# Four buffers for a head's exponentials, and the class key's column copied for two heads at once

## The reference

```
AC = einsum('bqhd,bkhd->bhqk', q + u, k)
BD = einsum('bqhd,khd->bhqk', q + v, kr)
prob = softmax((AC + BD) * inv_sqrt_d, axis=-1)
vec = einsum('bhqk,bkhd->bqhd', prob, val).reshape(b, s_len, H * DH)
h = layer_norm(h + vec @ W_o[i], ln1_g[i], ln1_b[i])
ff = relu(h @ W_ff1[i] + b_ff1[i]) @ W_ff2[i] + b_ff2[i]
h = layer_norm(ff, ln2_g[i], ln2_b[i])
```

## Time and profile before

| what | value |
|---|---|
| median of 3 runs | 2653.75 us (2649.84 to 2658.7) |
| the profiled execution's own time | 2649.49 us |
| its span | 2647.7 us |
| mean granted TensorE clock | 0.968 |
| busy: PE, DVE, ACT, POOL | 84%, 70%, 61%, 45% |
| calls of line 1676 | 512 |

### The profile page before, as it was taken

How to read it: one execution, slowest core, us unless ns; L and a number is a source line. 1 busy time by engine, 2 the same in 40 slices (tenths; PEclk the granted TensorE clock), 3 DMA queues, 4 the chain that set the end, 5 groups by cost and what they waited for, 6 DMA issues and landing times. The chain is left out here.

```text
span 2647.7 us, 61352 instructions
## 1 busy us (share of the span) xinstructions
PE 2226.1 (84%) x19254; PEld 1636.3 (62%) x19254; DVE 1844.0 (70%) x5666; ACT 1611.5 (61%) x5073; POOL 1188.7 (45%) x2205
## 2 busy tenths in 40 slices
PE   0159999999988999999899999999899989972998
PEld 0136666666766666667666666676666666651565
DVE  8837777777767777777677777777677777773333
ACT  2136666666666677676666777666576666661222
POOL 3025555555556555545565555545455555511011
PEclk9679999999999999999999999999999999996999
DMA  4344444445554444455544444546444444406110
GB/s 162 95 124 115 110 106 106 106 117 135 138 153 118 107 105 107 103 145 140 148 122 103 101 105 106 122 131 183 109 95 102 102 103 93 97 24 205 49 41 27
DMA packets 378062, 295.38 MB, mean 112 GB/s; under 512 B 45087, under 2 KB 350721, under 8 KB 376739
## 3 DMA queue, kind: packets, MB, share of 16 engines
q1 hardware_dynamic: 370603, 272.41, 41.5%
q10 hardware_dynamic: 4864, 12.68, 1.4%
q0 software_dynamic: 2272, 6.35, 0.7%
HBM read 137.71 MB, written 72.07 MB: 79 GB/s over the span
## 5 line engine op out<-in xcount | busy, mean ns | idle before, releaser
L1654 ACT ACTIVATE E<-E,nb 128x257 f32<-128x257 f32 x1024 | 517.3, 518 | 40.8 <-DVE nb L1837 40.2
L1837 DVE CUSTOM_DVE_ANT_0 E<-bk,cb 128x257 f32<-128x257 f32 x1024 | 390.3, 419 | 75.3 <-PE bk L1447 73.9
L1354 PE MATMUL bk<-hin,w_sb 128*128 128x257 f16 x3072 | 423.9, 275 | 11.8 <-ACT rel L1589 7.0
L1799 DVE TENSOR_TENSOR pt<-bk,pt 128x512 f16<-128x512 f32 x512 | 353.9, 691 | 77.0 <-ACT pt L1639 70.2
L1402 PE MATMUL bk<-ident,E 128*128 128x128 f32 x2048 | 324.1, 281 | 68.4 <-ACT E L1654 52.5
L1354 PEld LDWEIGHTS bk<-hin,w_sb 128*128 128x128 f16 x3072 | 298.0, 98 | 62.7 <-issue 10.3
L1402 PEld LDWEIGHTS bk<-ident,E 128*128 128x128 f32 x2048 | 220.4, 141 | 156.7 <-ACT E L1654 135.5
L1639 ACT ACTIVATE pt<-bk 128x512 f16<-128x512 f32 x512 | 311.3, 608 | 6.9 <-PE bk L1402 6.9
L1290 POOL TENSOR_SCALAR wf<-wf 128x256 f32<-128x256 f32 x216 | 93.9, 435 | 426.7 <-DMA wf<-in_w_dram 258.2
L1446 PE MATMUL bk<-kh,qs 128*128 128x257 f16 x1024 | 255.2, 275 | 10.8 <-DMA kl<-rk 10.6
L1240 POOL TENSOR_SCALAR rq<-rel 128x257 f16<-128x257 f32 x248 | 101.3, 409 | 342.3 <-ACT rel L1589 342.3
(11 more groups left out here) (303 smaller groups left out, 4474.7 us busy)
## 6 DMA issues: line engine op xcount, KB each, us to landing
qs<-rq SPq DMA_DIRECT2D x256, 128.5 KB
kh<-rk SPq DMA_DIRECT2D x256, 128.5 KB
kl<-rk SPq DMA_DIRECT2D x256, 128.5 KB
wf<-in_w_dram SPq DMA_DIRECT2D x168, 128.0 KB, 2.9
w_split_dram<-wh SPq DMA_DIRECT2D x168, 128.0 KB, 2.2
xs_dram<-in_c_blank_dram SPq DMA_DIRECT2D x24, 772.5 KB
w_sb<-w_split_dram SPq DMA_DIRECT2D x18, 1024.0 KB, 15.2
wf<-in_we_dram SPq DMA_DIRECT2D x96, 128.0 KB, 2.6
```

The lines of the kernel that those rows point to most:

```text
L1354: r_ = mm(bank[4 + s % 2][:, 0:S], wcol(a, C_QKV, k, 3 * HD, chunk_at(s)), hin[:, m, k, :], start=i == 0, stop=i == 5)
L1654: act.activation(E[:, h % 2, qt, :], E[:, h % 2, qt, :], ACT.Exp, bias=nb[:, 2 * h + qt:2 * h + qt + 1], scale=-1.0, accum_out=sums[:, qt, ...
L1799: v.tensor_tensor(pt[:, h, 1, :, 0:IMG], bank[2 + h % 2][:, :].rearrange("p (k s) -> p k s", k=QT), pt[:, h, 0, :, 0:IMG], ALU.subtract).t ...
L1837: v.tensor_tensor_reduce(E[:, h % 2, qt, :], bank[qt][:, 0:S], cb[:, h, :], -SCORE, 3e38, ALU.add, ALU.min, nb[:, 2 * h + qt:2 * h + qt + ...
```

## The change

`E` gets `EB = 4` buffers in place of two, indexed by `h % EB`. The copy of the class key's column is made only at odd h, for heads h - 1 and h together, with one instruction in place of two: twelve elements for each partition instead of six. Its semaphore `ecol_ok` counts to 8 for each pass instead of 16. DVE's wait ahead of overwriting a buffer moves from head h - 2 to head h - 4.

```diff
+EB = 4
...
-        E = sb("E", [P, 2, QT, S])
+        E = sb("E", [P, EB, QT, S])
...
-                                         E[:, h % 2, qt, kt * P:(kt + 1) * P], ident[:, :])
+                                         E[:, h % EB, qt, kt * P:(kt + 1) * P], ident[:, :])
...
-                pe.wait_ge(ecol_ok, at(16, 16))
+                pe.wait_ge(ecol_ok, at(8, 8))
...
-                        act.activation(E[:, h % 2, qt, :], E[:, h % 2, qt, :], ACT.Exp, bias=nb[:, 2 * h + qt:2 * h + qt + 1],
+                        act.activation(E[:, h % EB, qt, :], E[:, h % EB, qt, :], ACT.Exp, bias=nb[:, 2 * h + qt:2 * h + qt + 1],
...
-                    act.wait_ge(e_ok, at(32, 2 * h + 2))
-                    act.activation(ecol[:, :, class_row(h, 0):class_row(h, 3):4], E[:, h % 2, :, CLS:S].broadcast_to([P, QT, 3]), ACT.Copy).then_inc(ecol_ok, 1)
+                    if h % 2:
+                        act.wait_ge(e_ok, at(32, 2 * h + 2))
+                        both = E[:, (h - 1) % EB:(h - 1) % EB + 2, :, CLS].rearrange("p b k -> p k b").unsqueeze(2).broadcast_to([P, QT, 3, 2])
+                        first, i = class_row(h - h % 4, 0), (h - 1) % 4
+                        act.activation(ecol[:, :, first:first + 12].rearrange("p k (c i) -> p k c i", i=4)[:, :, :, i:i + 2], both, ACT.Copy).then_inc(ecol_ok, 1)
...
-                    if h >= 2:
-                        v.wait_ge(t_done, at(16, h - 1))
-                        v.wait_ge(ecol_ok, at(16, h - 1))
+                    if h >= EB:
+                        v.wait_ge(t_done, at(16, h - EB + 1))
+                        v.wait_ge(ecol_ok, at(8, (h - EB) // 2 + 1))
...
-                        v.tensor_tensor_reduce(E[:, h % 2, qt, :], bank[qt][:, 0:S], cb[:, h, :], -SCORE, 3e38,
+                        v.tensor_tensor_reduce(E[:, h % EB, qt, :], bank[qt][:, 0:S], cb[:, h, :], -SCORE, 3e38,
```

## The result

The changed kernel took 2640.07 us as the median of 6 runs (2638.91 to 2643.75), the kernel before 2655.5 us in the runs beside it; the ratio is 0.9945 with a 95% interval of 0.9931 to 0.9959. That is 0.55% less, some 14.6 us (0.0055 x 2655.5), bounds 10.9 and 18.3. The profiled execution has a span of 2637.1 us against 2647.7.

A forecast was written before the change was run, and what follows sets the result against it. ACT, gapless in the MIDDLE head loop, was taken as the bound; savings of 14.3 + 0.65 + 1.4 + 0.3 + 2.5 + 0.3 = 19.5 us took the median of 2653.75 to 2634 us, range 2626 to 2648.

The forecast's parts named there:

- 0.75 us in a MIDDLE pass: Head loop of a MIDDLE pass: fifteen copies of 0.10 us become seven of 0.105, saving 0.75 us, 14.3 over 19 loops.
- head 14 loss: MIDDLE head loop at head 14, where DVE makes three reciprocals first: 0.07 us of room, about 0.02 us of saving lost.
- 0.47 and more elsewhere: MIDDLE head loop: DVE's score tile is ready 0.47 us or more before ACT takes it, at heads other than 14.
- OPENING 0.65: OPENING pass: 0.65 us saved, one slot less because DVE is on the path at heads 1 and 2.
- ENTRY 1.4: Three ENTRY passes: 0.47 us each from five copies fewer ahead of PE's wait for POOL's class rows, 1.4 us in all.
- CLOSING 0.3: Three CLOSING passes, where PE is the bound: 0.1 us saved in each, 0.3 in all.
- TAIL 2.5: Five TAIL passes with routing: slots saved up to head 11, less those DVE's routing eats, give 0.5 us each, 2.5 together.
- FINAL 0.3: FINAL pass: the same as TAIL passes with routing but with less slack, 0.3 us saved.
- Behind the loop nothing reads what changed, so each saving is handed on: Second halves of passes, after the head loop: compute chains of the same length, so loop savings reach the total undiminished.
- another engine takes over: Rival, chance 0.16: DVE's or PE's slack runs out in MIDDLE loops, half the saving remains, some 9 us: 2645 us.
- Slower: Rival, chance 0.05: ACT is held for the pair copy's full 0.27 us, 10.5 us lost over some 27 passes: 2664 us.
- page's price: Rival, chance 0.02: each call removed frees 0.3 us, or its whole 0.218 us duration, 56 us over 32 passes: 2598 us.

## Why the prediction was right, and by how much it was off

I predicted 2634 us, 19.5 us less than the median then known, and measured is a ratio that makes it 14.6 less, with bounds of 10.9 and 18.3. That is inside the range of 2626 to 2648 us, but just short of the forecast case itself (15 to 24 us saved).

- *ACT is the bound of the loop, and a copy costs the distance between starts.* Right, in MIDDLE loops. Two heads went from 3.48 to 3.38 us, the pair copy has 0.10 to 0.11 us. Doubling it and leaving it out moved the MIDDLE loops by +0.72 and -0.67 us.
- *0.75 us in a MIDDLE pass.* Measured 0.72. The new slot was forecast exactly (0.105), the old one rounded up: with its median of 0.097, fifteen old copies less seven new ones are 15 x 0.097 - 7 x 0.105 = 0.72, not 0.76. The head 14 loss came as foreseen: its slack fell from 0.10 to 0.04 us. 19 loops gave 14.0 for 14.3. The prediction's slack of "0.47 and more elsewhere" was a misreading: in the pass of the earlier trace rows DVE was ahead by 0.16 us at head 1 and 0.35 at head 4. Head 1 has 0.07 left after the change, so it did no harm.
- *The buffers alone are worth nothing.* Shown for the MIDDLE loops (31.11 us); that they are needed for the pairing, too (35.33 without). Not so in the first CLOSING loop of the execution, which is 0.3 us longer with them. Over the whole kernel the interval leaves 0.23% faster to 0.01% slower.
- *OPENING 0.65, ENTRY 1.4, CLOSING 0.3, TAIL 2.5, FINAL 0.3.* OPENING can't be told: its loop took 42.0 and 42.7 us before, 41.6, 43.7, 41.8 and 41.7 after. ENTRY passes gave 2.6 with a spread from drops larger than that; loops without a drop, of 36.3 or 36.4 us before, take 35.8: some 0.6 less each, for the 0.47 of the sum. CLOSING gave -0.2: two of three loops stay at 34.4 us with and without the change, as PE's being the bound would have it, and the first grew by 0.3. TAIL gave 1.9, and its loops 0.37 each for 0.5. FINAL's loop took 29.34 us against 29.84 and 30.59.
- *Behind the loop nothing reads what changed, so each saving is handed on.* This step failed, in part. The MIDDLE second halves grew by 4.7 us in sum, a third of what the loops had given: 2.8 by the steady 0.15 us a pass, whose cause stays open, and the rest by clock drops, whose number I can't tie to the change. Without this the forecast would have been 19.5 - 4.7 = 14.8 us. That this meets the 14.6 is in part luck, as the other terms' errors cancel: ENTRY gave 1.2 more than forecast, CLOSING and TAIL 1.1 less.

Of the rivals, "another engine takes over" is hardly seen even with the copies gone altogether (0.05 us, most of it at head 14). "Slower" would have needed a slot of 0.21 us. The "page's price" was no price for this instruction from the start: the Trainium skill ("ScalarE: Activation LUTs", rules for kernel authors) gives its budget of about 0.3 us for an ACTIVATE whose bias is a `[128,1]` pointer operand, a condition that the prediction left out, and the copy has no bias. The doubled copy measured 0.103 in a queue that is never empty.

## What to carry to other kernels

Take the price of a small instruction on a full engine from start to next start, not from its duration: here 0.10 for 0.22 us. Join such instructions where that engine sets the pace, and look which buffer the joined one keeps occupied: with two buffers the joined copy made the loop 4.2 us longer, with four 0.72 shorter. A saving in one stage is not wholly a saving of the kernel, even where the dependences seem to hand it on: compare the other stages over several profiles before you explain it.

## What the runs showed that I had not expected

- Executions of one kernel, with the same work, differ by drops of the granted clock to 0.50, which cost 1.5 us each in a MIDDLE pass. In 32 of the 36 ENTRY passes of the twelve profiles there is at least one, at the class rows or at the wait for the values.
- POOL is busy 45% of the span, yet eight copies of 0.20 us each in a loop where it is busy 22.5 of 31 us became a wait for DVE, and, put earlier, one for ACT: its own chain of layer norm steps had no room for them between heads 3 and 8 in either place that was tried.
